# Two-layer graph attention on one core: the projections of a pair parted at other places, the end written in the loop's order, evictions reordered

## Chip, cores, metric

One Trainium2 chip, one NeuronCore. The metric is device time in microseconds of one execution; the profile is one execution, taken by the hardware profiler.

## The reference

128 graphs of 128 nodes with 256 features. Layer 0: `x = x + adj @ (h @ W0) + b0`. Layer 1 is an 8-head graph attention. In both, `h = max(layernorm(x), 0)`.

```python
feat_proj = (feats @ fc_w + fc_b).reshape(bs, n, HEADS, dim).transpose(0, 2, 1, 3)
q = feat_proj @ q_w + q_b
k = feat_proj @ k_w + k_b
logits = q + jnp.swapaxes(k, -1, -2)
masked = logits + (1.0 - adj_mat[:, None]) * NEG
masked = jax.nn.leaky_relu(masked, negative_slope=0.01)
attn = jax.nn.softmax(masked, axis=-1)
out = attn @ feat_proj
out = out.transpose(0, 2, 1, 3).reshape(bs, n, HEADS * dim)
out = out @ fp_w + fp_b + feats
return jax.nn.sigmoid(out)
```

## The kernel before

The graphs are taken in 64 pairs. At the start (begin(), `fold`) fc_w and fp_w are multiplied into one matrix per head, so that each pair needs `g = h @ m` (8 heads of 256 columns for each of its two graphs) and then `y = sum over heads of attn @ g`. Every fp32 product is written as three matmuls of split operands (high and low part, `split`, L400 to L405), and every result that is an operand later is evicted twice: its high part by ScalarE (ACT: `g_high`, `last_high`, `pT_high`, `hT_high`, `ah_high`), its low part by VectorE (DVE: `g_low`, `last_low`, `pT_low`, `hT_low`, `ah_rest`).

Names of a pair's work. `aggregate` (L449) and `transform` make layer 0's output; `residual0`, `stats1`, `mean1` and GpSimd's `variance1` to `shift1` and ACT's `h1_relu` make h; `transpose_h` turns it. `last_head` multiplies the eighth head together with the key and query columns; j is the graph of the pair. `turn_keys` transposes the keys, DVE's `key_rows_out` copies them (L855), SyncE (SP) writes them to DRAM (`keys_out`) and reads them back into all partitions (`keys_in`, L303); GpSimd's (POOL) `mask_keys` (L1617) adds the mask, DVE's `mask_min` (L881) the query, then `leaky` (L888), ACT's `exp` (L1300), DVE's `inverse`, POOL's `normalise` (L1624), PE's `transpose_p` (L521), `pT_high` and `pT_low`, and PE's `attend`, each for one graph j and one half c of the heads. DVE's `add_feats`, ACT's `tanh` and `sigmoid`, POOL's `residual1` and SP's `store` end a pair.

The projections of a pair are six pieces of 512 columns, A0, A1, A2 of the first graph and B0, B1, B2 of the second, six matmuls each (36 in all), and SIXTH, 12 matmuls of 256 columns. They share four PSUM banks in turn (`RING`, L43): a piece can start when `g_low` or `last_low` of the bank's tenant before it is done (`ring_free`). The tenants of one bank follow each other so: B0 and A0; A1 and B1; A2 and SIXTH; THERE (the second graph's last_head of the pair after) and B2. The transposed attention has one bank (`TRING`): each `transpose_p` waits for the `pT_low` before it.

Every engine's program is a hand-written list, executed in order: begin(), then step(i, q) in a loop over pairs (PE, DVE, ACT for i = 4 to 60, POOL 5 to 58, SP 6 to 59; three steps in one turn of the loop), then finish(). Between engines there are only semaphores. The step of PE: L656 to L678.

Of the kernel before, what the change touches and what calls it, by code (L numbers as in the profile page):

```python
# [12 lines left out]
DT = D // P  # L13
# [5 lines left out]
BANK = 512  # L19
# [22 lines left out]
LAST = (HERE, THERE)  # L42
RING = ((B0, -1), (A1, 0), (A2, 0), (THERE, 1), (A0, 0), (B1, 0), (SIXTH, 0), (B2, 0))  # L43
# [4 lines left out]
def gnn_pair(nc, graph, identity, head_mask, row_coef, w0, bias0, fc_wT, fc_b, qk_w, q_b, k_b, fp_w, fp_b, out):  # L48
# [9 lines left out]
    with ExitStack() as ctx:  # L58
# [188 lines left out]
        def _(sp):  # L247
# [119 lines left out]
            def finish():  # L367

                keys_in(59, 2, 0)
                keys_in(59, 2, 1)  # L370
                load(63, 0)
                keys_out(60, 0)
                store(57)
                keys_in(60, 0, 0)
                keys_in(60, 0, 1)
                keys_out(61, 1)
                store(58)
                keys_in(61, 1, 0)
                keys_in(61, 1, 1)
                keys_out(62, 2)  # L380
                store(59)
                keys_in(62, 2, 0)
                keys_in(62, 2, 1)
                keys_out(63, 0)
                keys_in(63, 0, 0)
                keys_in(63, 0, 1)
                store(60)
# [11 lines left out]
        def _(pe):  # L399
            def split(out_ap, pairs, first=True, last=True):  # L400

                terms = [(w, m) for (wh, wl), (mh, ml) in pairs for w, m in ((wl, mh), (wh, ml), (wh, mh))]
                for n, (w, m) in enumerate(terms):
                    mm = pe.matmul(out_ap, w, m, start=first and n == 0, stop=last and n == len(terms) - 1)  # L404
# [91 lines left out]

            def project(p, q, n):
                bank = ring_free(n, p)
                folded(p)
                j, s = n // 3, slice(n % 3 * BANK, (n % 3 + 1) * BANK)  # L500
                split(bank[:],
                      [((hT_hi[q][:, dt, j, :], hT_lo[q][:, dt, j, :]), (m_hi[:, dt, s], m_lo[:, dt, s]))
                       for dt in range(DT)]).then_inc(pe_g[n], 1)
# [37 lines left out]
            def begin():  # L541
# [109 lines left out]
                transform(5, 2)  # L651
                attend(3, 0, 0, 0)
# [3 lines left out]
            def step(i, q):  # L656
                project(i - 1, (q + 2) % U, B0)
                attend(i - 1, (q + 2) % U, 0, 1)
                transpose_h(i + 1, (q + 1) % U)
                project(i, q, A1)  # L660
# [5 lines left out]
                project(i, q, A0)  # L666
                attend(i - 1, (q + 2) % U, 1, 0)
# [3 lines left out]
                project(i, q, B1)  # L671
# [3 lines left out]
                project(i, q, B2)  # L675
# [4 lines left out]
            def finish():  # L680

                h_ready(60)
                project(60, 0, B0)
                attend(60, 0, 0, 1)
                h_ready(61)
                project(61, 1, A1)
                transpose_p(60, 1, 1)
                transpose_h(62, 2)
# [4 lines left out]
                project(61, 1, A0)  # L693
                attend(60, 0, 1, 0)
                transpose_p(61, 0, 0)
                attend(60, 0, 1, 1)
                turn_keys(62, 2)
                project(61, 1, B1)
                transform(63, 0)
                sixth_heads(61, 1)  # L700
                transpose_p(61, 0, 1)
                project(61, 1, B2)
                attend(61, 1, 0, 0)
                transpose_p(61, 1, 0)
                project(61, 1, B0)
# [1221 lines left out]
```

## Time and profile before

| | us |
|---|---|
| median of 3 runs | 1433.05 (1432.97 to 1435.38) |
| the profiled execution | 1436.59 |
| its span, first to last instruction | 1434.8 |
| its mean granted clock of PE | 0.994 |

In the rows below PE is TensorE, a time is counted from the span's start, a line is that of the kernel before, and `[x <-E tile Ln]` behind an instruction is the engine's idle time ahead of it and what ended it. `x4` behind a merged row counts instructions. A matmul's own duration is longer than its distance to the next, because matmuls are pipelined: distances of starts are what adds up.

### The profile page before, as it was taken

Reading aid. Unit: us, or ns where it says so; the run is one execution under the profiler, and the core shown is the slowest. Engines: PE = TensorE matmul, PEld = TensorE weight load, DVE = VectorE, ACT = ScalarE, POOL = GpSimd, SP = SyncE. Lnnn points to the kernel's source line nnn. Section 1 sums busy time; section 2 is a strip of 40 time slices with the busy share of each in tenths; the row PEclk is TensorE's granted clock in tenths of the full one; section 3 lists DMA queues with packets and bytes.
Section 4 is the critical chain, followed back from the end, with each engine's and each line's share of the span. In section 5 each row is a group of like instructions: output and inputs, shape, how many; then the busy total and the mean of one; then the engine's idle time right before and its main releaser. Section 6 shows DMA issues by size and latency. Waiting matters only on the chain.

```text
span 1434.8 us, 32663 instructions
## 1 busy us (share of the span) xinstructions
PE 1408.9 (98%) x9624; PEld 1296.5 (90%) x9624; DVE 1267.8 (88%) x4536; ACT 1100.5 (77%) x3428; POOL 1105.1 (77%) x1291
## 2 busy tenths in 40 slices
PE   9989999999999999999999999999999999999987
PEld 7878999999999999999999999999999999998876
DVE  7978999999999999999999999999999989998865
ACT  4757877877877877877877877877877877877755
POOL 4768888787787788787788788788778778778744
PEclk9989999999999999999999999999999999999999
DMA  6321332232232232232232231232232232231111
GB/s 223 103 61 63 95 103 69 85 103 70 84 103 67 87 103 71 83 103 69 85 103 69 85 103 70 84 103 72 82 103 71 83 103 74 80 103 61 58 41 56
DMA packets 43245, 123.13 MB, mean 86 GB/s; under 512 B 5968, under 2 KB 9680, under 8 KB 43216
## 3 DMA queue, kind: packets, MB, share of 16 engines
q1 hardware_dynamic: 42928, 122.77, 26.9%
q8 instruction: 13, 0.21, 0.1%
q14 instruction: 16, 0.13, 0.0%
q10 hardware_dynamic: 288, 0.01, 0.0%
HBM read 105.46 MB, written 17.30 MB: 86 GB/s over the span
## 4 chain that ended last, share of the span: by engine, by line
PE 90%; POOL 3%; DVE 3%; issue 2%; DMA 1%; ACT 1%; POOLq 0%; ACTq 0%; DVEq 0%
PE gbank L404 43%; PE ybank L404 23%; PE bank L404 9%; PE tbank L521 7%; PE bank L449 4%; PE bank L479 2%; PE gbank L424 1%; POOL att L1624 1%; POOL att L1617 1%; DVE att L881 1%; DMA late<-key_rows 1%; PE bank L457 0%; DVE g_lo L864 0%; DVE att L888 0%; DMA qk<-qk_w_dram 0%
## 5 line engine op out<-in xcount | busy, mean ns | idle before, releaser
L1617 POOL TENSOR_TENSOR att<-late,t_pos 128x512 f32<-128x512 f32 x256 | 331.1, 1295 | 175.6 <-PE tbank L521 117.0
L1300 ACT ACTIVATE att<-att 128x128 f32<-128x128 f32 x1024 | 397.8, 393 | 50.0 <-DVE att L888 49.7
L404 PE MATMUL gbank<-m_hi,hT_lo 128*128 128x512 f32 (+1 forms) x1024 | 402.4, 393 | 2.1 <-DVE g_lo L864 2.1
L404 PE MATMUL gbank<-m_hi,hT_hi 128*128 128x512 f32 (+1 forms) x1024 | 375.0, 366 | 0.0
L404 PE MATMUL gbank<-m_lo,hT_hi 128*128 128x512 f32 (+1 forms) x1024 | 373.2, 364 | 0.0
L1624 POOL TENSOR_TENSOR att<-att,rinv 128x512 f32<-128x512 f32 x256 | 295.0, 1152 | 63.4 <-DVE rinv L893 63.2
L881 DVE TENSOR_SCALAR_CACHE_REDUCE att<-att,kq_sb 128x128 f32<-128x128 f32 x1024 | 291.5, 341 | 33.1 <-POOL att L1617 32.8
L864 DVE TENSOR_TENSOR g_lo<-gbank,g_hi 128x512 fp32r<-128x512 f32 x448 | 302.5, 679 | 18.2 <-ACT g_hi L1293 14.4
L1307 ACT ACTIVATE pT_hi<-tbank 128x512 fp32r<-128x512 f32 x256 | 152.7, 597 | 178.4 <-PE tbank L521 175.5
L1293 ACT ACTIVATE g_hi<-gbank 128x512 fp32r<-128x512 f32 x448 | 258.7, 592 | 38.7 <-PE gbank L404 38.5
L404 PE MATMUL ybank<-g_hi,pT_lo 128*128 128x256 f32 x889 | 249.7, 281 | 4.4 <-DVE g_lo L864 4.3
L404 PE MATMUL ybank<-g_lo,pT_hi 128*128 128x256 f32 x889 | 249.1, 280 | 0.0
L404 PE MATMUL ybank<-g_hi,pT_hi 128*128 128x256 f32 x889 | 248.8, 280 | 0.0
L404 PEld LDWEIGHTS gbank<-m_hi,hT_hi 128*128 128x128 f32 x1024 | 192.9, 188 | 34.2
L404 PEld LDWEIGHTS gbank<-m_hi,hT_lo 128*128 128x128 f32 x1024 | 193.8, 189 | 21.0 <-DVE g_lo L864 2.3
L404 PEld LDWEIGHTS gbank<-m_lo,hT_hi 128*128 128x128 f32 x1024 | 194.6, 190 | 19.9
L871 DVE TENSOR_TENSOR pT_lo<-tbank,pT_hi 128x512 fp32r<-128x512 f32 x256 | 173.3, 677 | 37.1 <-ACT pT_hi L1307 37.1
L1300 ACT ACTIVATION_READ_ACCUMULATOR att<-att 128x1 f32 x1024 | 194.8, 190 | 0.0
L888 DVE SCALAR_TENSOR_TENSOR att<-att 128x516 f32<-128x516 f32 x256 | 191.4, 766 | 0.1
L404 PEld LDWEIGHTS ybank<-g_hi,pT_lo 128*128 128x128 f32 x889 | 167.4, 188 | 13.0 <-issue 5.4
L404 PEld LDWEIGHTS ybank<-g_lo,pT_hi 128*128 128x128 f32 x889 | 167.4, 188 | 7.6
L404 PEld LDWEIGHTS ybank<-g_hi,pT_hi 128*128 128x128 f32 x889 | 166.9, 188 | 0.0
(123 smaller groups left out, 2876.9 us busy)
## 6 DMA issues: line engine op xcount, KB each, us to landing
late<-key_rows SPq DMA_DIRECT2D x128, 512.0 KB, 6.3
g_in<-graph_dram SPq DMA_DIRECT2D x64, 512.0 KB, 3.3
out_dram<-ends SPq DMA_DIRECT2D x63, 256.0 KB, 6.6
att<-fc_wT_dram SPq DMA_DIRECT2D x4, 256.0 KB, 5.8
late<-fp_w_dram SPq DMA_DIRECT2D x4, 256.0 KB, 5.3
ends<-fp_w_dram SPq DMA_DIRECT2D x2, 512.0 KB, 7.7
late<-fc_wT_dram SPq DMA_DIRECT2D x2, 512.0 KB, 8.4
key_rows<-rows SPq DMA_DIRECT2D x64, 8.0 KB, 1.4
```

Of the source, the lines that this page charges most:

```text
L404: mm = pe.matmul(out_ap, w, m, start=first and n == 0, stop=last and n == len(terms) - 1)
L449: mm = pe.matmul(sums[:, j, dt, :], h0_f[q][:, j, dt * P:(dt + 1) * P], adjT_of(q)[:, j, :], start=True, stop=True)
L521: mm = pe.transpose(tbank[:, h * P:(h + 1) * P], att[j][c][:, h * P:(h + 1) * P], ident[:])
L864: dve.tensor_tensor(piece(g_lo, n), bank_of(n, p), piece(g_hi, n).bitcast(F32), ALU.subtract)\
L871: dve.tensor_tensor(pT_lo[j][:, hs, :], rows, pT_hi[j][:, hs, :].bitcast(F32), ALU.subtract)\
L881: r = dve.tensor_scalar(a[:, s], a[:, s], kq_sb[q][:, 1, j, c * HC + h:c * HC + h + 1], None, ALU.add, ALU.min, accum_out=a[:, CH + h:CH + ...
L888: dve.scalar_tensor_tensor(out=a, in0=a, scalar=SLOPE, in1=a, op0=ALU.mult, op1=ALU.min)\
L1293: act.activation(piece(g_hi, n), bank_of(n, p), ACT.Copy).then_inc(a_g[n], 1)
L1300: e = act.activation(a[:, s], a[:, s], ACT.Exp, scale=-1.0, bias=a[:, CH + h:CH + h + 1], accum_out=esum[j][c][:, h:h + 1])
L1307: act.activation(pT_hi[j][:, c * HC:(c + 1) * HC, :], rows, ACT.Copy).then_inc(a_pT[NC * j + c], 1)
L1617: gp.tensor_tensor(a, keys[q][:, j, c * HC:(c + 1) * HC, :], t_pos[q][:, j, :].unsqueeze(1).broadcast_to([P, HC, P]), ALU.add)\
L1624: gp.tensor_tensor(a, a, rinv[j][c][:].unsqueeze(2).broadcast_to([P, HC, P]), ALU.mult)\
```

## The change

`split` takes a slice of its terms, and `project_part(p, q, n, first, stop)` issues the terms first to stop−1 of a piece's six matmuls; only the part that ends at 6 signals. Each part asks for the bank and for the folded weights as `project` does. In the loop the pieces are parted so: two matmuls of B0 go ahead of attend(i, 0, 0) (and aggregate, transpose_p(i, 1, 0)); one of A1 ahead of attend(i−1, 0, 1) and transpose_h; one of B1 ahead of attend(i−1, 1, 0), attend(i−1, 1, 1), turn_keys and transpose_p(i, 0, 0); two of B2 ahead of sixth_heads, transform and transpose_p(i, 0, 1). The rest of the piece follows where the whole one stood. DVE's step has g_low(i, A1) and pT_low(i−1, 1, 1) ahead of the keys' work, and last_low(i+1, 1) right behind keys_queries(i+1, 1). ACT's has g_high(i, A1) and pT_high(i−1, 1, 1) first. POOL's and SP's steps are unchanged. In begin() PE has B0(3) parted, DVE the work around pair 2 in another order, ACT last_high(3, 0, 1) ahead of exp(2, 0, 1). finish() of all five engines is written in the order of the step, with what no longer exists left out.

The diff, cut to the parts that are spoken of (finish() is shown for PE's first pair, and for SP):

```diff
@@ sync, finish
+                load(63, 0)
                 keys_in(59, 2, 0)
                 keys_in(59, 2, 1)
-                load(63, 0)
+                store(57)
                 keys_out(60, 0)
-                store(57)
                 keys_in(60, 0, 0)
                 keys_in(60, 0, 1)
+                store(58)
                 keys_out(61, 1)
-                store(58)
...
@@ tensor
-            def split(out_ap, pairs, first=True, last=True):
+            def split(out_ap, pairs, first=True, last=True, part=slice(None)):
 
                 terms = [(w, m) for (wh, wl), (mh, ml) in pairs for w, m in ((wl, mh), (wh, ml), (wh, mh))]
-                for n, (w, m) in enumerate(terms):
+                for n, (w, m) in list(enumerate(terms))[part]:
...
+            def piece_terms(q, n, out_ap, part):
+                j, s = n // 3, slice(n % 3 * BANK, (n % 3 + 1) * BANK)
+                return split(out_ap,
+                             [((hT_hi[q][:, dt, j, :], hT_lo[q][:, dt, j, :]), (m_hi[:, dt, s], m_lo[:, dt, s]))
+                              for dt in range(DT)], part=part)
+
+            def project_part(p, q, n, first, stop):
+                bank = ring_free(n, p)
+                folded(p)
+                mm = piece_terms(q, n, bank[:], slice(first, stop))
+                if stop == TERMS:
+                    mm.then_inc(pe_g[n], 1)
...
@@ tensor, begin
                 transform(5, 2)
+                project_part(3, 0, B0, 0, 2)
                 attend(3, 0, 0, 0)
...
             def step(i, q):
-                project(i - 1, (q + 2) % U, B0)
+                project_part(i - 1, (q + 2) % U, B0, 2, 6)
+                project_part(i, q, A1, 0, 1)
                 attend(i - 1, (q + 2) % U, 0, 1)
                 transpose_h(i + 1, (q + 1) % U)
-                project(i, q, A1)
+                project_part(i, q, A1, 1, 6)
                 transpose_p(i - 1, 1, 1)
...
                 project(i, q, A0)
+                project_part(i, q, B1, 0, 1)
                 attend(i - 1, (q + 2) % U, 1, 0)
                 attend(i - 1, (q + 2) % U, 1, 1)
                 turn_keys(i + 1, (q + 1) % U)
                 transpose_p(i, 0, 0)
-                project(i, q, B1)
+                project_part(i, q, B1, 1, 6)
+                project_part(i, q, B2, 0, 2)
                 sixth_heads(i, q)
                 transform(i + 2, (q + 2) % U)
                 transpose_p(i, 0, 1)
-                project(i, q, B2)
+                project_part(i, q, B2, 2, 6)
+                project_part(i, q, B0, 0, 2)
                 attend(i, q, 0, 0)
...
             def finish():
 
-                h_ready(60)
-                project(60, 0, B0)
+                project_part(60, 0, B0, 2, 6)
+                project_part(61, 1, A1, 0, 1)
                 attend(60, 0, 0, 1)
-                h_ready(61)
-                project(61, 1, A1)
+                transpose_h(62, 2)
+                project_part(61, 1, A1, 1, 6)
                 transpose_p(60, 1, 1)
-                transpose_h(62, 2)
                 project(61, 1, A2)
...
@@ vector, begin
                 mask_min(2, 2, 0, 1)
                 mask_min(2, 2, 0, 0)
-                leaky(2, 0, 1)
                 leaky(2, 0, 0)
-                mask_min(2, 2, 1, 0)
                 hT_low(3, 0)
                 pT_low(1, 1, 1)
+                leaky(2, 0, 1)
+                mask_min(2, 2, 1, 0)
                 mask_min(2, 2, 1, 1)
                 inverse(2, 0, 0)
-                g_low(2, A1)
-                ah_rest(4, 1)
-                add_feats(1, 1)
-                inverse(2, 0, 1)
-                leaky(2, 1, 1)
                 keys_queries(3, 0, 0)
                 keys_queries(3, 0, 1)
                 last_low(3, 0, 0)
+                g_low(2, A1)
+                ah_rest(4, 1)
+                leaky(2, 1, 1)
+                inverse(2, 0, 1)
+                add_feats(1, 1)
+                key_rows_out(3)
                 leaky(2, 1, 0)
-                key_rows_out(3)
                 g_low(2, A2)
...
@@ vector, step
                 mask_min(i, q, 1, 1)
+                g_low(i, A1)
+                pT_low(i - 1, 1, 1)
                 keys_queries(i + 1, (q + 1) % U, 0)
                 last_low(i + 1, (q + 1) % U, 0)
                 inverse(i, 0, 0)
                 leaky(i, 0, 1)
                 keys_queries(i + 1, (q + 1) % U, 1)
-                pT_low(i - 1, 1, 1)
-                g_low(i, A1)
+                last_low(i + 1, (q + 1) % U, 1)
                 mask_min(i, q, 1, 0)
...
                 pT_low(i, 0, 0)
-                last_low(i + 1, (q + 1) % U, 1)
                 g_low(i, A0)
...
@@ scalar, begin
                 last_high(3, 0, 0)
+                last_high(3, 0, 1)
                 exp(2, 0, 1)
-                last_high(3, 0, 1)
...
@@ scalar, step
             def step(i, q):
+                g_high(i, A1)
+                pT_high(i - 1, 1, 1)
                 g_high(i, A2)
                 last_high(i + 1, (q + 1) % U, 0)
-                pT_high(i - 1, 1, 1)
-                g_high(i, A1)
                 last_high(i + 1, (q + 1) % U, 1)
```

## Rows read from the trace of the kernel before

**Rows 1.** The page, part 1: busy us (share of span) xinstructions of every engine.
```profile
PE 1408.9 (98%) x9624; PEld 1296.5 (90%) x9624; DVE 1267.8 (88%) x4536; ACT 1100.5 (77%) x3428; POOL 1105.1 (77%) x1291
```

**Rows 2.** Chain of waits, 120 to 1290 us: shares by engine, tile and line.
```profile
by line: PE gbank L404 48.7%; PE ybank L404 26.4%; PE bank L404 10.1%; PE tbank L521 8.1%; PE bank L449 4.2%; PE bank L479 2.0%; PE bank L457 0.5%
```

**Rows 3.** Stretches: us, busy of PE, PEld, DVE, ACT, POOL; granted clock, DMA share, GB/s.
```profile
1272.62:1294.11 21.49, 21.49 (x152) 19.89 (x151) 19.54 (x71) 17.05 (x53) 17.27 (x21) 1.00 0.31 86
...
1294.11:1317.26 23.15, 21.66 (x151) 19.86 (x151) 19.54 (x71) 17.12 (x53) 19.81 (x22) 1.00 0.19 68
...
1338.75:1361.20 22.45, 22.16 (x151) 19.75 (x151) 19.95 (x71) 16.69 (x53) 14.52 (x17) 1.00 0.18 60
...
1361.20:1390.04 28.84, 24.42 (x144) 21.76 (x143) 19.00 (x65) 16.46 (x53) 15.39 (x16) 0.88 0.12 46
...
1390.04:1434.80 44.76, 36.19 (x244) 32.31 (x242) 27.77 (x87) 26.00 (x86) 18.49 (x17) 0.99 0.16 48
```

**Rows 4.** Timeline of PE in begin(): start, us, instruction [idle before <- releaser].
```profile
83.36 0.60 PE L404 MATMUL bank<-n_hi,hT_lo 128*128 128x272 f32 x1 [3.53 <-DVE hT_lo L841]
...
92.48 0.37 PE L457 MATMUL bank<-ident,kq_sb 128*16 128x128 f32 x1 [2.04 <-DVE last_lo L859]
...
111.73 0.39 PE L404 MATMUL bank<-n_hi,hT_lo 128*128 128x272 f32 x1 [1.38 <-DVE hT_lo L841]
```

**Rows 5.** Stretch 85 to 86 us, columns as in Rows 3 (granted clock behind POOL).
```profile
85.00:86.00 1.00, 1.00 (x6) 1.00 (x5) 1.00 (x3) 0.88 (x4) 0.87 (x1) 0.50 0.72 272
```

**Rows 6.** Timeline of PE in one step of the loop.
```profile
705.21 1.05 PE L449 MATMUL bank<-g_in,h_f 128*128 128x128 f32 x8
...
706.10 0.60 PE L521 MATMUL tbank<-ident,att 128*128 128x128 f32 x4
...
706.46 0.48 PE L404 MATMUL gbank<-m_hi,hT_lo 128*128 128x512 f32 x1
...
707.93 0.28 PE L404 MATMUL ybank<-g_hi,pT_lo 128*128 128x256 f32 x1
...
709.35 0.60 PE L479 MATMUL bank<-ident,h 128*128 128x128 f32 x4
...
713.00 0.28 PE L404 MATMUL bank<-n_hi,hT_lo 128*128 128x272 f32 x1
...
713.74 0.29 PE L404 MATMUL gbank<-n_hi,hT_lo 128*128 128x272 f32 x1
```

**Rows 7.** Timeline of DVE in the same step.
```profile
707.37 0.69 DVE L871 TENSOR_TENSOR pT_lo<-tbank,pT_hi 128x512 fp32r<-128x512 f32 x1 [0.46 <-ACT pT_hi L1307]
...
711.02 0.68 DVE L841 TENSOR_TENSOR hT_lo<-bank,hT_hi 128x512 fp32r<-128x512 f32 x1
...
713.27 0.35 DVE L881 TENSOR_SCALAR_CACHE_REDUCE att<-att,kq_sb 128x128 f32<-128x128 f32 x1 [0.51 <-POOL att L1617]
...
714.87 0.85 DVE L888 SCALAR_TENSOR_TENSOR att<-att 128x516 f32<-128x516 f32 x1
...
719.84 0.27 DVE L855 COPY rows<-bank 16x128 f32<-16x128 f32 x1
```

**Rows 8.** DVE, ACT and POOL in begin() (timelines); then a piece of the chain.
```profile
78.19 3.45 DVE L888 SCALAR_TENSOR_TENSOR att<-att 128x516 f32<-128x516 f32 x2
...
79.04 0.60 ACT L1285 ACTIVATE hT_hi<-bank 128x512 fp32r<-128x512 f32 x1
...
79.36 1.72 POOL L1607 TENSOR_TENSOR xb<-g_in,b_row 128x512 f32<-128x512 f32 x1
...
81.64 1.06 DVE att L881 x8
```

**Rows 9.** Timeline of PE: its last matmul.
```profile
1430.19 0.28 PE L404 MATMUL bank<-last_hi,pT_hi 128*128 128x256 f32 x1
```

**Rows 10.** Timeline of POOL: mask_keys of the two steps after Rows 7.
```profile
728.24 1.29 POOL L1617 TENSOR_TENSOR att<-late,t_pos 128x512 f32<-128x512 f32 x1 [1.44 <-DMA late<-key_rows]
...
748.95 1.28 POOL L1617 TENSOR_TENSOR att<-late,t_pos 128x512 f32<-128x512 f32 x1 [0.66 <-DMA late<-key_rows]
```

More of the change, by code:

```diff
@@ L499, in project @@
                 folded(p)
[L500 to L503, printed above, removed]
+                piece_terms(q, n, bank[:], slice(None)).then_inc(pe_g[n], 1)
+            def project_part(p, q, n, first, stop):
[4 more added lines that the diff above has]
+                    mm.then_inc(pe_g[n], 1)
             def sixth_heads(p, q):
@@ L1144, in finish @@
             def finish():
-                mask_min(61, 1, 0, 1)
                 g_low(60, SIXTH)
@@ L1153, in finish @@
                 leaky(61, 0, 0)
-                mask_min(61, 1, 1, 0)
                 hT_low(62, 2)
-                leaky(61, 1, 0)
-                leaky(61, 0, 1)
-                inverse(61, 0, 0)
+                mask_min(61, 1, 0, 1)
+                mask_min(61, 1, 1, 1)
+                g_low(61, A1)
                 pT_low(60, 1, 1)
@@ L1192, in finish @@
-                inverse(62, 0, 0)
                 keys_queries(63, 0, 0)
                 last_low(63, 0, 0)
+                inverse(62, 0, 0)
+                leaky(62, 0, 1)
                 keys_queries(63, 0, 1)
-                g_low(62, A1)
+                last_low(63, 0, 1)
+                mask_min(62, 2, 1, 0)
+                inverse(62, 0, 1)
                 g_low(62, A2)
-                mask_min(62, 2, 1, 1)
                 add_feats(61, 1)
                 key_rows_out(63)
-                last_low(63, 0, 1)
@@ L1222, in finish @@
                 leaky(63, 0, 1)
                 mask_min(63, 0, 1, 0)
+                inverse(63, 0, 1)
+                g_low(63, A2)
+                add_feats(62, 2)
                 leaky(63, 1, 0)
-                inverse(63, 0, 1)
-                mask_min(63, 0, 1, 1)
+                leaky(63, 1, 1)
                 pT_low(63, 0, 0)
-                leaky(63, 1, 1)
+                g_low(63, A0)
                 inverse(63, 1, 0)
-                g_low(63, A0)
-                add_feats(62, 2)
@@ L1232, in finish @@
-                inverse(63, 1, 1)
                 pT_low(63, 0, 1)
                 g_low(63, B1)
+                g_low(63, SIXTH)
+                inverse(63, 1, 1)
                 pT_low(63, 1, 0)
-                g_low(63, SIXTH)
                 g_low(63, B0)
```

209 lines of the change are left out of this document (111 added, 98 removed).

## Prediction

> **What bounds the kernel now.** First the page: TensorE (PE) is busy 1408.9 of 1434.8 us, 98% [rows 1]. That is an average over three stages, so next the chain of waits between 120 and 1290 us: every line named there is PE's [rows 2]. Then the stretches cut at one fixed point of every step, the start of `last_head(…, 1)`: a step of the loop is 21.49 us long with PE busy 21.49 [rows 3]. In the loop PE never waits; only fewer or shorter PE instructions, or a new wait, could change it. The idle time is at the two ends. In the loop's last steps and behind it PE stands idle (length less busy) 1.5 us in the step that ends at 1317.26, 0.3 in the one that ends at 1361.20, 4.4 in the next and 8.6 in the final stretch (4.3 of that is the tail), and the clock column reads 0.88 in one of them [rows 3]. In begin() PE waits 3.53 us at 83.36 and 1.38 at 111.73 for hT_lo, and 2.04 at 92.48 before turn_keys [rows 4]. The first of these also costs clock: 85 to 86 is at 0.50, that is 1.2 GHz [rows 5].
>
> **Part 1: the parted projections in the loop, 0.** The same 36 matmuls, weight loads and boundaries remain. A projection behind a transposition takes 1.47 us (706.46 to 707.93) [rows 6], and five blocks of 512 columns still follow a transposition per step; five times a 512-column run is still followed by a 256- or 272-column one. So nothing is saved and nothing added on PE. What moves is the filler between: before attend(i−1, 0, 1) and attend(i−1, 1, 0) one matmul of the next piece is put (0.23 us, a sixth of 1.39), before sixth_heads and attend(i, 0, 0) two (0.46). The pieces end when they did; attends, transform, aggregate and transposes in between start 0.23 or 0.46 later. The added waits are repeats, or ask earlier for a bank: B1's head asks for g_low(A1) ahead of two attends instead of behind them, B2's head for last_low(…, 1) before sixth_heads. The diff brings both forward on VectorE (DVE). Queued behind such a wait would be all of PE.
>
> I walk one new step through the queues to see whether one of these becomes a wait. transpose_p(1, 0) is 0.46 later, so pT_low ends and mask_min(0, 0) starts 0.46 later than in [rows 7]; hT_low, at 711.02 to 711.70, ends at about 712.15, and PE wants it at 713.00 [rows 6]: 0.85 left of 1.3. DVE idles 0.51 at 713.27, waiting for mask_keys(1, 1), which hangs on PE's transpose_p(1, 1), not moved; so the delay is swallowed there [rows 7]. Next come g_low(A1), done by about 715.0 where B1's head starts at 715.9 (713.74 + 0.76 + 1.39), and pT_low(1, 1), 0.6 later for an attend that starts at 717.5. leaky(0, 1) falls back by 1.2, so exp(0, 1) ends near 718.4 and DVE may wait some 0.3 for it at inverse(0, 1). With last_low(…, 1), 0.34 issue to issue, now in front, rows is copied some 0.5 later than 719.84 [rows 7]. g_low(A2) has 2 us left before sixth_heads, normalise(0, 0) on GpSimd (POOL), 1.0 later than now, 1.3 before its transposition. The smallest distance left is about 0.65 us. Hence 0 in all 57 steps; the bounds are 0 and, from the keys' loop below, +0.18 us a step.
>
> **Part 2: begin(), −7.8 us.** DVE's work for pair 2 is reordered. Now hT_low(3) is behind both leaky(2, 0, ·), 3.45 us for two, and mask_min(2, 1, 0), 1.06 [rows 8]. In the new order only leaky(2, 0, 0) is ahead of it: 78.19 plus half of 3.45 is 79.9, past the end of hT_hi at 79.64, so hT_lo (0.68, its last part overlapping) is there at 80.55 and PE goes on at 80.6 instead of 83.36. It has idled 0.9 us instead of 3.5. After 1.38 idle the row at 111.73 is followed by full speed, after 3.53 the clock was halved [rows 4, 5]; I take full clock. last_head ×2 and project(2, A0) take 2.9, attend 1.42: PE reaches turn_keys(3) at 84.9. Ahead of last_low(3, 0) DVE has pT_low, leaky(2, 0, 1) (1.7 again, beside POOL's input work), two mask_min, inverse and keys_queries: 81.1 + 1.7 + 2.1 + 0.25 + 0.35 = 85.5. So turn_keys runs at 85.65, against 92.48: 6.8 sooner. From there by the same durations: B1 waits for g_low(2, A1), 86.2; sixth_heads(2) for g_low(2, A2), which stands behind ah_rest, leaky, add_feats, rows and leaky, 89.5; B2 to 92.35; B0 94.2; attend(2, 0, 1) waits for g_low(SIXTH), 96.2; then A1, two transposes, A2 and an attend to 102.7; hT_low(4), behind mask_min, leaky, g_low, mask_min and pT_low, ends at 103.9. The wait before last_head(4, 0) remains (1.25 us), but the point is 103.95 instead of 111.73 [rows 4]: −7.8. POOL and the keys of pair 3 come 7.0 sooner or more. Bounds: −4 (the clock falls once more, 1.3 to 1.9, and the two waits behind turn_keys grow) and −9 (those waits vanish).
>
> **Part 3: finish() in the loop's order, −15.5 us.** POOL's and SyncE's (SP's) finish take over from step 59 on. If the loop's order holds there, steps 59 and 60 take 21.49. Step 61 lacks aggregate, 0.89 (705.21 to 706.10) [rows 6]: 20.6. Step 62 lacks transform too, 12 matmuls of 256 columns as in an attend, 1.42 (707.93 to 709.35): 19.2. PE's own work from the tail of B0(62) to the end, item by item in the new list (a matmul of 512 columns 0.23, attend and sixth_heads 1.42): 1.0 + 0.23 + 1.42 + 1.16 + 0.44 + 2.77 + 0.23 + 2.83 + 0.44 + 1.24 + 0.46 + 1.42 + 0.44 + 1.0 + 0.46 + 1.42 + 0.44 + 1.0 + 1.42 + 0.44 + 2.83 = 23.1, where 0.44 is four transposes with what the next 512 columns lose behind them. I add 0.35 because B1's head of pair 63 waits for g_low(63, A1): that pair's step is shorter and its keys come by DMA. 23.4. The last stage, from the end of the last attend, is untouched: 1430.47 to 1434.80, 4.3 [rows 9]. The start of step 58's B0 tail is 713.74 − 706.92 = 6.8 before its cut at 1294.11, 1287.3. Sum: 1287.3 + 3 × 21.49 + 20.6 + 19.2 + 23.4 + 4.3 = 1419.3 against 1434.8: −15.5. By stretches of [rows 3] that is 1.7 of the one to 1317.26, 1.0 of the one to 1361.20, 8.2 of the next (28.84 against 20.6) and 4.7 of the last. Bounds: −16 (no wait at all) and −11 (the last stretch keeps what it loses now).
>
> **The sum.** 1434.8 − 7.8 − 15.5 = 1411.5 us of span. The profiled run took 1436.59, 1.8 more than its span and 3.5 more than the median of 1433.05; the same difference of 23.3 taken from the median gives 1409.8, and that is the forecast.
>
> **Rivals.**
> (a) Begin's gain is mostly given back: the keys of pair 3 or a clock drop set PE's next stop. For it: three waits follow each other there, and I resolve them to about 0.5 us each. Against it: everything behind 92.48 hangs on DVE work that moves along. Begin then gives −2 and the time is 1415.6.
> (b) The keys' loop takes the step over. From the copy of rows to mask_keys 8.40 us (719.84 to 728.24) [rows 7, 10], mask_keys with the hand-over to DVE 1.33, DVE's work to the next copy 11.25 without its idle 0.51: 20.98. The change adds last_low 0.34 and up to 0.33 of waiting for exp: 21.67, 0.18 over 21.49. For it: the sum. Against it: 8.40 is not every step's: the next copy, 21.49 later at 741.33, is followed by mask_keys at 748.95, 7.62 [rows 10]; the mean of the two is 0.39 less. If it holds, 57 × 0.18 less the 0.9 of distance is +9: 1419.
> (c) Slower: leaky(0, 1), (1, 0) and (1, 1) land on POOL's normalise and mask_keys. In the loop leaky(0, 1) takes 0.85 [rows 7], in begin() beside POOL's input work 1.7 each, while POOL's xb takes 1.72 [rows 8]. Were all four of a step to take 1.7, DVE would need up to 4 us more; it has 1.95 of idle (21.49 − 19.54) [rows 3]. It decides from 1.95 + 23.3/57 = 2.36 us a step on; at 3 us a step the loop gives +60, the total 1470. Against it: in [rows 7] leaky meets POOL already and loses 0.25.
> (d) The orders outside the loop do nothing, since the ends wait for DMA: 1433.
>
> By the Trainium skill (SBUF — State Buffer, "Who interferes with whom") a DVE instruction with two SBUF inputs and a GpSimd instruction that reads SBUF exclude each other, and the later one blocks for the whole of the other. leaky is such an instruction, and 1.7 us in [rows 8] agree in kind. By that rule each overlap could cost up to one POOL instruction, 1.3 us, which is rival (c).
>
> **Chances.** Forecast 0.70 (own range 1405 to 1416), (a) 0.11, (b) 0.11, (c) 0.06, (d) 0.02. The range leaves out (c), (d) and the far ends of the others: 1404 to 1421. About 0.2% (3 us) is what a measurement of this kernel can tell from no change. Faster by more 0.92, within it 0.02, slower by more 0.06.
>
> **What would show it.** In the profile after: the loop's step still 21.49 with PE busy 21.49; if it is longer, the idle row names hT_lo or g_lo at `last_head` or at B1's head, and POOL's wait for late<-key_rows near zero would show (b), leaky above 1.2 us (c). The wait for hT_lo near 80 under 1.2 us, turn_keys(3) near 85.7 and last_head(4, 0) near 104 show part 2. Idle of PE behind the loop, the tail aside, of about 0.4 us instead of 10.5 shows part 3, and its clock full until the end. The forecast is wrong if one of the distances of part 1, 0.65 us at the least, is used up in every step, or if the last pairs' keys, 6 us on their way, stop PE in step 62 or 63.

## The result, and the profile after

| | before | after |
|---|---|---|
| median, us | 1433.36 (1432.97 to 1435.38, 4 runs) | 1397.97 (1397.29 to 1399.49, 4 runs) |
| the profiled execution | 1436.59 | 1399.49 |
| its span | 1434.8 | 1397.7 |

The ratio is 0.975 (95% interval 0.9735 to 0.9769): 35.4 us less, where 23.3 were forecast. 1398 lies outside the range of 1404 to 1421.

The page of the kernel after, part 1, against [rows 1]:

```profile
PE 1386.2 (99%) x9624; PEld 1276.7 (91%) x9624; DVE 1289.3 (92%) x4536; ACT 1092.9 (78%) x3428; POOL 1123.7 (80%) x1291
```

PE's waits in it for hT_lo, the normalised attention, g_lo and last_lo (us in total, times, longest):

```profile
PE bank L405 <- DVE hT_lo L867: 2.6, 3, 1.4
...
PE tbank L532 <- POOL att L1650: 0.7, 2, 0.5
PE gbank L405 <- DVE g_lo L890: 0.6, 1, 0.6
PE bank L458 <- DVE last_lo L885: 0.2, 1, 0.2
```

PE has the same 9624 matmuls and is busy 22.7 us less with them. That is the first sign: idle time that is removed leaves the busy time as it is.

Where the 37.1 us of span went. The timeline of PE in begin(), kernel after, beside [rows 4]:

```profile
80.74 0.39 PE L405 MATMUL bank<-n_hi,hT_lo 128*128 128x272 f32 x1 [0.81 <-DVE hT_lo L867]
...
85.15 0.27 PE L458 MATMUL bank<-ident,kq_sb 128*16 128x128 f32 x1
...
103.45 0.39 PE L405 MATMUL bank<-n_hi,hT_lo 128*128 128x272 f32 x1 [1.43 <-DVE hT_lo L867]
```

And the stretches of the kernel after, cut at the starts of last_head(…, 1) (columns as in [rows 3]):

```profile
1251.92:1273.15 21.23, 21.23 (x151) 19.64 (x150) 19.93 (x71) 16.92 (x55) 17.57 (x21) 1.00 0.29 87
1273.15:1294.39 21.24, 21.24 (x152) 19.65 (x150) 19.93 (x71) 16.95 (x55) 17.56 (x21) 1.00 0.29 87
...
1315.62:1336.85 21.23, 21.23 (x151) 19.65 (x150) 19.21 (x66) 16.93 (x55) 17.41 (x20) 1.00 0.19 63
1336.85:1357.20 20.35, 20.35 (x144) 18.77 (x143) 18.89 (x66) 15.71 (x52) 15.97 (x17) 1.00 0.21 66
1357.20:1397.70 40.50, 35.61 (x245) 32.25 (x243) 28.86 (x93) 27.17 (x88) 20.11 (x18) 0.98 0.16 47
...
84.00:86.00 2.00, 2.00 (x16) 1.80 (x15) 2.00 (x9) 0.48 (x4) 1.24 (x2) 1.00 0.87 223
```

- Begin: last_head(4, 0) at 103.45 instead of 111.73, 8.3 sooner. The clock is 1.00 where it was 0.50 [rows 5].
- Loop: from there to the start of last_head(59, 1) at 1293.94 (the cut of [rows 3] at 1294.11 lies 0.17 behind it) were 1182.2 us, in 55 steps; to the same point at 1273.15 are 1169.7 now. 12.5 less. The usual step is 21.23 instead of 21.49, with PE busy in all of it, before and after.
- End: 140.9 us were left, 124.55 are. 16.3 less.

8.3 + 12.5 + 16.3 = 37.1. The loop's 12.5 is what the forecast had at nothing.

In the loop no wait is gone, since there was none [rows 3]. The same matmuls stand closer together. The timeline of PE in one step of the kernel after: sixth_heads from 727.57, transform from 728.93, transpose_p, B2's tail and B0's head, attend(i, 0, 0) from 732.11, the aggregate, and in the next step attend(i−1, 0, 1), the one of [rows 6], from 736.02:

```profile
727.34 0.39 PE L405 MATMUL gbank<-m_lo,hT_hi 128*128 128x512 f32 x1
727.57 0.28 PE L405 MATMUL gbank<-m_hi,hT_lo 128*128 128x256 f32 x1
...
728.93 0.28 PE L405 MATMUL bank<-w_hi,ah_lo 128*128 128x256 f32 x1
...
730.30 0.60 PE L532 MATMUL tbank<-ident,att 128*128 128x128 f32 x4
730.65 0.47 PE L405 MATMUL gbank<-m_hi,hT_hi 128*128 128x512 f32 x1
...
732.11 0.28 PE L405 MATMUL ybank<-g_hi,pT_lo 128*128 128x256 f32 x1
...
733.52 1.05 PE L450 MATMUL bank<-g_in,h_f 128*128 128x128 f32 x8
...
736.02 0.28 PE L405 MATMUL ybank<-g_hi,pT_lo 128*128 128x256 f32 x1
...
737.38 0.60 PE L480 MATMUL bank<-ident,h 128*128 128x128 f32 x4
```

Twelve matmuls of 256 columns took 1.42 in [rows 6] (707.93 to 709.35). Here they take 1.36 in attend(i−1, 0, 1), in sixth_heads and in transform, but 1.41 in attend(i, 0, 0). The two attends on graph 1, 24 matmuls, take 2.72 instead of 2.82 (743.92 to 746.64, against 715.88 to 718.70). So 60 of the 72 matmuls of 256 columns in a step go at 113.3 ns from start to start instead of 117.8, and 60 × 4.5 ns = 0.27 is the step's 0.26.

What sets the pace shows in the matmuls of 512 columns ahead. The rows round to 10 ns; the trace has the starts in ns. The distances from each 512-column matmul to what follows it, where not said otherwise behind four transpositions, and the pace of the 256-column run behind (one group for each; the entry, the first two or three distances, varies from step to step):

```
before, attend(i-1,0,1), 6 ahead:  318 232 237 231 232 226            -> 117.8
after,  attend(i-1,0,1), 5 ahead:  319 231 237 232 231                -> 113.3
before, sixth_heads,     6 ahead:  317 235 230 231 226 229            -> 117.8
after,  sixth_heads,     7 ahead:  319 235 229 231 226 229 232        -> 113.3
after,  attend(i,0,0),   6 ahead:  313 226 229 231 226 229            -> 117.8
before, attend(i,0,0),   6 ahead:  318 235 229 232 226 229            -> 117.8
after,  attend(i-1,1,*), 7 ahead:  232 226 229 232 226 229 231 (no transposition between) -> 113.3
```

The distances fall into a beat of three, 226, 229, 232 ns. Where the last one is 231 or 232, the 256-column run behind it goes at 113.3; otherwise at 117.8. A run keeps its pace to its end: 12 matmuls in a row, or 24.

The theory for the experiments: it is the number of 512-column matmuls between the last transposition and a 256-column run, taken in this beat, that sets the run's pace. Before, all cuts were at the ends of pieces of six, and a six always ended on the wrong beat: of the four runs in each of 54 steps of the loop none was fast. After, three of the four are fast in 53 or 54 steps, and attend(i, 0, 0) in none. Its rivals: parity (odd counts fast), the neighbours (what VectorE, ScalarE and GpSimd read and write meanwhile), any parting at all, the new order of the evictions, and the ends.

### The profile page after: what moved, and what is told of

The parts are those of the page before. It is cut to its first block, busy times and chain, and to the rows that moved or that the text cites. A ratio compares the mean times of both kernels' runs of the same rounds, so it can differ in the third digit from the quotient of the medians.

```text
span 1397.7 us, 32661 instructions
## 1 busy us (share of the span) xinstructions
PE 1386.2 (99%) x9624; PEld 1276.7 (91%) x9624; DVE 1289.3 (92%) x4536; ACT 1092.9 (78%) x3428; POOL 1123.7 (80%) x1291
## 4 chain that ended last, share of the span: by engine, by line
PE 93%; POOL 2%; DVE 2%; issue 2%; ACT 1%; DMA 0%; POOLq 0%; ACTq 0%; DVEq 0%
PE gbank L405 45%; PE ybank L405 23%; PE bank L405 10%; PE tbank L532 8%; PE bank L450 4%; PE bank L480 2%; PE gbank L425 1%; POOL att L1650 1%; POOL att L1643 1%; DVE att L907 1%; PE bank L458 0%; ACT att L1326 0%; DMA qk<-qk_w_dram 0%; DVE att L914 0%; ACT g_hi L1319 0%
## 5 line engine op out<-in xcount | busy, mean ns | idle before, releaser
L405 PE MATMUL gbank<-m_hi,hT_hi 128*128 128x512 f32 (+1 forms) x1024 | 383.1, 374 | 0.0
L405 PE MATMUL gbank<-m_hi,hT_lo 128*128 128x512 f32 (+1 forms) x1024 | 378.6, 370 | 0.6 <-DVE g_lo L890 0.6
L405 PE MATMUL gbank<-m_lo,hT_hi 128*128 128x512 f32 (+1 forms) x1024 | 379.1, 373 | 0.0
L1650 POOL TENSOR_TENSOR att<-att,rinv 128x512 f32<-128x512 f32 x256 | 290.7, 1136 | 82.2 <-DVE rinv L919 81.9
L1319 ACT ACTIVATE g_hi<-gbank 128x512 fp32r<-128x512 f32 x448 | 255.0, 585 | 6.5 <-PE gbank L405 6.4
L914 DVE SCALAR_TENSOR_TENSOR att<-att 128x516 f32<-128x516 f32 x256 | 209.8, 838 | 0.1
```

What stands on the lines that cost most here:

```text
L914: dve.scalar_tensor_tensor(out=a, in0=a, scalar=SLOPE, in1=a, op0=ALU.mult, op1=ALU.min)\
L1319: act.activation(piece(g_hi, n), bank_of(n, p), ACT.Copy).then_inc(a_g[n], 1)
L1650: gp.tensor_tensor(a, a, rinv[j][c][:].unsqueeze(2).broadcast_to([P, HC, P]), ALU.mult)\
```

## The beat measured by itself

The changed kernel with a row of matmuls behind its end, all other engines idle:

```diff
+            def bench():
+                for n in list(range(10)) + list(range(9, -1, -1)):
+                    turn4()
+                    wide(n)        # n matmuls of 512 columns
+                    half()         # 12 matmuls of 256 columns
+                for n in range(1, 10):
+                    wide(n)
+                    half()
...
             finish()
+            bench()
```

> The changed kernel with a row of matmuls appended on PE once everything else is done (other engines idle, no waits inside): groups of four transposes, n matmuls of 512 columns, 12 matmuls of 256 columns, for n = 0 to 9 and back, then other orders; the appended part is not to be counted in the time. It measures the distance of the 256-column matmuls, 113.3 ns in the runs after 5 and 7 matmuls in the loop of the changed kernel and 117.8 ns everywhere in the loop of the kernel before. Theory, beat of three: in runs of 512-column matmuls the distances repeat as 226, 229, 232 ns, and a 256-column run goes at 113.3 ns if it begins behind a 232, at 117.8 otherwise; so behind four transposes n = 4 and 7 are fast, 5, 6 and 8 slow, and without transposes every third n is fast. Rival, parity: odd n fast, even n slow. Rival, neighbours: the distance is set by what the other engines read and write meanwhile, so with all of them idle every run shows the same distance, whatever n.

The stretch of the first loop but for its last run (columns as above):

```profile
1409.40:1465.30 55.90, 55.90 (x395) 51.97 (x394) 0.00 (x0) 0.00 (x0) 0.00 (x0) 1.00 0.00 1
```

From the timeline the groups without transpositions, n = 1, 2 and 3 (L788 is a matmul of 512 columns, L794 one of 256):

```profile
1467.14 0.39 PE L788 MATMUL gbank<-m_hi,hT_lo 128*128 128x512 f32 x1
1467.36 0.28 PE L794 MATMUL ybank<-g_hi,pT_lo 128*128 128x256 f32 x1
...
1468.78 0.39 PE L788 MATMUL gbank<-m_hi,hT_lo 128*128 128x512 f32 x1
1469.01 0.39 PE L788 MATMUL gbank<-m_lo,hT_hi 128*128 128x512 f32 x1
1469.24 0.28 PE L794 MATMUL ybank<-g_hi,pT_lo 128*128 128x256 f32 x1
...
1470.60 0.39 PE L788 MATMUL gbank<-m_hi,hT_lo 128*128 128x512 f32 x1
```

No other engine is busy, the clock is 1.00, and both paces are there: 1467.36 to 1468.78 is 1.42, 1469.24 to 1470.60 is 1.36. That ends the neighbours' theory. In ns, without a transposition between the groups:

```
n  distances of the n matmuls              12 x 256 behind
1  226                                     117.8
2  230 231                                 113.3
3  226 229 232                             113.4
4  226 229 232 225                         117.8
5  229 232 225 230 231                     113.3
6  226 229 232 226 229 232                 113.3
7  225 230 231 226 229 232 226             117.8
8  229 232 226 229 231 226 229 232         113.4
9  226 229 232 226 229 231 226 229 232     113.4
```

Behind a fast group the beat starts at 225 or 226, behind a slow one at 229 or 230 (the first row stands behind a run that itself followed transpositions); a run is fast when the count ends it at 231 or 232. That makes six of nine counts fast, not every third, as I had expected: each run's pace moves the start of the next beat. Every third it is where the start stays the same: behind last_head's 272-column matmuls, where the first distance is always 231 or 232, n = 1, 4 and 7 are fast (113.3 to 113.4), 2, 3, 5, 6 and 8 slow (117.7 to 118.0). Parity is out: 3 and 5 are fast, 1 and 7 slow, 2, 6 and 8 fast. The operands are out too: with one and the same weights and columns in all n matmuls, 4 and 7 are fast, 3, 5, 6 and 8 slow. With four transpositions ahead the first distance is 312 to 319 and the beat comes in at different places:

```
entry 312..313:  313 226 229 232 226 229       n = 4 fast, 3 and 6 slow
entry 315..316:  316 226 233 236 229 232       n = 6 fast, 4 and 5 slow
entry 318, 235:  318 235 229 232 226 229 232   n = 4 and 7 fast, 3, 5, 6 and 8 slow
entry 319, 231:  319 231 237 232 231 226 229   n = 5 fast, 3 and 7 slow
```

So "n = 4 and 7 are fast, 5, 6 and 8 slow" was only half right: the entry depends on what went before the transpositions, and n = 4, 5, 6 and 7 were each seen fast and slow. What holds, with few exceptions, is the rule on the last distance. Over the thirteen traces here (twelve kernels, the changed one twice) there are 3307 runs of eight or more 256-column matmuls behind two or more of 512: with a last distance of 231 to 233, 1617 of 1654 were fast; with any other, 23 of 1653. Three of the exceptions stand in this bench, behind 318, 232, 237, 231 and twice behind 316, 226, 233. 60 matmuls of 256 columns in a row, begun slow, stayed at 117.8 to the end.

## The loop, the ends, and any parting at all

The loop's part of the change alone, on the kernel before (step() of PE, DVE and ACT; B0's first two matmuls of pair 3 in begin() so that the loop can start):

```diff
 begin, PE of the kernel before
+                project_part(3, 0, B0, 0, 2)
                 attend(3, 0, 0, 0)
 finish, PE of the kernel before
-                project(60, 0, B0)
+                project_part(60, 0, B0, 2, 6)
```

> The kernel before with only the loop's part of the change: step() of TensorE, VectorE and ScalarE as in the changed kernel, and B0's two first matmuls of pair 3 ahead of attend(3, 0, 0); begin() and finish() of every engine otherwise as before. Theory (four of the five groups of 256-column runs of a step run at 113.3 instead of 117.8 ns a matmul, 60 matmuls): a step takes 21.23 instead of 21.49 us, 57 steps give 14.8, so about 1418.5 us. The forecast's theory (nothing saved in the loop): 21.49 a step, 1433. Rival, the step is shorter only because the ends start it in another rhythm: 1433 too, with 21.49 a step here.

Measured: 1421.83 us (1418.92 to 1425.75, 5 runs), ratio 0.9905 (0.9875 to 0.9934), 13.6 us less by the ratio; a step is 21.23. The loop alone makes the loop's gain.

Its profile says two things more. Begin() is the old one, yet last_head(4, 0) stood at 105.90 in this execution, not at 111.73: the wait for hT_lo ended at 81.44 after 2.42 us, and the clock stayed up (timeline of PE, then a stretch, columns as above):

```profile
81.44 0.40 PE L405 MATMUL bank<-n_hi,hT_lo 128*128 128x272 f32 x1 [2.42 <-DVE hT_lo L857]
```

```profile
84.00:86.00 2.00, 2.00 (x15) 1.74 (x13) 0.32 (x1) 0.70 (x4) 0.40 (x1) 1.00 0.94 326
```

So of begin's 8.3 us in the profiles some 5.8 belong to a late and half-clocked stretch that not every execution has. And from the start of last_head(59, 0) the loop's last steps with the old finish() take 146.3 us to the end, where they took 141.6 in the profile of before. PE's wait for the normalised attention in the first of its steps is 2.08 instead of 1.49. Part of what the loop gains is given back there.

The complement, begin() and finish() as changed, step() of PE, DVE and ACT as before:

> The complement: the changed kernel with step() of TensorE, VectorE and ScalarE as before, and B0 of pair 3 and of pair 60 whole; begin() and finish() as changed. Theory: begin gives 8 (turn_keys(3) at about 85, last_head(4, 0) at about 103.5), finish 13 to 14, the loop keeps 21.49 a step: about 1412 us. By the forecast's theory this is the whole change: 1433.4 - 23.3 = 1410. If the ends gave the whole of the measured 35 us by setting the loop's rhythm: 1398.

Measured: 1412.32 us (1411.92 to 1413.14, 4 runs), ratio 0.9839 (0.9806 to 0.9871), by the ratio 23.1 less than before beside it; a step is 21.49; last_head(4, 0) stands at 103.07. These are the parts that the forecast had in its sum, at the size it had them. Beside finish()'s 16.3 that leaves some 7 us for begin(), an estimate from these figures: the old begin()'s late stretch seems to be in most executions, though it was not in the profiled one of the loop alone. The two halves, 13.6 and 23.1, give 36.7; the whole is 35.4, well within what their intervals leave open.

All four heads two matmuls long:

```diff
-                project_part(i, q, A1, 0, 1)
+                project_part(i, q, A1, 0, 2)
...
-                project_part(i, q, B1, 0, 1)
+                project_part(i, q, B1, 0, 2)
```

> The changed kernel with two matmuls of the next piece ahead at all four places (B0 2, A1 2, B1 2, B2 2), in the loop and in the ends; one matmul more ahead than now for A1 and B1, nothing else. Counts of 512-column matmuls since the last transposition ahead of a 256-column run: 6, 8 behind last_head, 6 and 6, where the changed kernel has 5, 7, 7 and 6. Theory (the count decides whether a run goes at 113.3 or 117.8 ns): all runs slow, 21.49 a step, 1398 + 15 = 1413 us. Rival, any parting of the pieces shortens the step (shorter groups of 512 columns, filler between): 21.23, 1398 us. Rival, the reordered evictions do it: 21.23, 1398 us.

Measured: 1412.29 us (1411.76 to 1413.39, 4 runs), ratio 0.9837 (0.9804 to 0.9869). One matmul more ahead at two places, and the loop's gain is gone: 21.49 a step. It isn't the parting, but where it cuts. The profile shows all groups slow, with 6, 8, 6 and 6 ahead.

Nothing parted, evictions and ends in the new order:

```diff
-                project_part(i - 1, (q + 2) % U, B0, 2, 6)
-                project_part(i, q, A1, 0, 1)
+                project(i - 1, (q + 2) % U, B0)
...
-                project_part(i, q, B1, 0, 1)
```

> The changed kernel with nothing parted: all pieces whole, in loop and ends; the new order of evictions and of the ends stays. Theory (the order of evictions gives nothing by itself, the counts are 6 everywhere): 21.49 a step, about 1412.5 us. Rival (the evictions' order gives the loop's gain): 21.23, 1398.

Measured: 1412.83 us (1412.16 to 1413.28, 4 runs), ratio 0.9844 (0.9827 to 0.9861). The new order of the evictions gives nothing by itself.

The stretches of one step in the middle of each of the four, the last line of the view (PE, then the other engines, busy):

```profile
sum 21.23, PE 21.23 PEld 19.64 DVE 19.95 ACT 16.94 POOL 17.57; mean PE 21.23 PEld 19.64 DVE 19.95 ACT 16.94 POOL 17.57
```

```profile
sum 21.48, PE 21.48 PEld 19.89 DVE 19.53 ACT 17.05 POOL 17.25; mean PE 21.48 PEld 19.89 DVE 19.53 ACT 17.05 POOL 17.25
```

```profile
sum 21.49, PE 21.49 PEld 19.90 DVE 19.95 ACT 16.93 POOL 17.61; mean PE 21.49 PEld 19.90 DVE 19.95 ACT 16.93 POOL 17.61
```

```profile
sum 21.48, PE 21.48 PEld 19.89 DVE 19.93 ACT 17.11 POOL 17.55; mean PE 21.48 PEld 19.89 DVE 19.93 ACT 17.11 POOL 17.55
```

They are the loop alone, the ends alone, all heads two, and whole pieces, in this order. PE is busy all of the step in each; only the length differs.

## What the order of the evictions is for

The changed kernel with the loop's evictions in the old order (VectorE's step is shown, ScalarE's goes back likewise):

```diff
 vector, step
-                g_low(i, A1)
-                pT_low(i - 1, 1, 1)
                 keys_queries(i + 1, (q + 1) % U, 0)
...
+                pT_low(i - 1, 1, 1)
+                g_low(i, A1)
-                last_low(i + 1, (q + 1) % U, 1)
...
                 pT_low(i, 0, 0)
+                last_low(i + 1, (q + 1) % U, 1)
```

> The changed kernel with VectorE's and ScalarE's step() as in the kernel before: the pieces parted as in the change, the loop's evictions in the old order. B1's head asks for g_low(A1), which in the old order ends 1.1 us behind the point where the head stands (716.97 against 715.88 in the step shown of before), and B2's head for last_low(..., 1), which ends at 722.4 where the head stands at about 720.2, 721.3 with the first wait. Theory (order of the evictions is what keeps the new parts free of waits): two waits of about 1.1 us each in every step, some 23.4 us a step, the total near 1520; the 256-column runs behind a wait may lose the fast pace too. Rival (the parts need no new order, the old one has slack): 21.23 a step, 1398.

PE's longest waits in its profile:

```profile
PE gbank L405 <- DVE last_lo L885: 82.1, 57, 1.7
PE gbank L405 <- DVE g_lo L890: 58.4, 58, 1.0
```

Measured: 1580.04 us (1579.64 to 1580.39, 4 runs), ratio 1.101 (1.0993 to 1.1031). The two waits are the expected ones, 1.0 and 1.4 us a step. I had 1520: the step is 24.44, 3.2 more than 21.23, not 2.2. Beside the 2.45 of idle time, the distances at the two waits (1411 and 1887 ns at 712.5 and 718.6 us, where 229 would stand without one) are 0.33 longer than their idle time of 1.01 and 1.50, the matmul behind each has 340 ns to the next instead of 229 (0.22 for both), and the runs of 24 behind a wait mostly fell to the slow pace (48 × 4.5 ns = 0.22). A head ahead of time asks for its bank ahead of time; without the new order the change would have cost 146 us.

## Four other cuts

```diff
 five_seven, against the changed kernel
-                project_part(i, q, B0, 0, 2)
+                project_part(i, q, B0, 0, 3)
-                project_part(i, q, A1, 0, 1)
+                project_part(i, q, A1, 0, 2)
 four_eight: no head of B0, A1 0 to 2
 four_seven: B0 0 to 3, A1 0 to 1
 seven_four: no head of B0, A1 0 to 1
```

> The changed kernel with three matmuls of B0 instead of two ahead of attend(i, 0, 0) and two of A1 instead of one ahead of attend(i-1, 0, 1), in the loop and the ends. Counts since the last transposition ahead of the 256-column runs become 7 before attend(i, 0, 0), where it is 6 now, and 5, 7, 7 at the three others, as now. Theory, beat of three: the last slow run of the step, attend(i, 0, 0), goes fast as well, 12 matmuls by 4.5 ns, 0.055 a step: 21.18 us, total about 1395. The parity rival expects the same here. If the fast pace went with the operands or the place in the step and not with the count: 1398.

> The changed kernel with no matmul of B0 ahead of attend(i, 0, 0) and two of A1 ahead of attend(i-1, 0, 1): B0 whole, B2 and B1 parted as now. Counts since the last transposition: 4 before attend(i, 0, 0), 8 before attend(i-1, 0, 1), 7 and 7 at the others. Theory, beat of three: behind the entry that the trace shows for four transposes and the aggregate (318, 232, 237, 231, 232, then 226, 229, 232), the eighth distance is a 232, and the fourth in attend(i, 0, 0)'s (313, 226, 229, 232) as well: all five places fast, 21.18 a step, about 1395 us. Rival, parity: both even, both slow, 21.28 a step, about 1401 us.

Measured: 1397.11 us (1395.97 to 1397.89, 4 runs), ratio 0.9735 (0.9718 to 0.9753), for 7 and 5; and 1396.03 (1395.48 to 1396.87, 4 runs), ratio 0.973 (0.9713 to 0.9748), for 4 and 8. A step is 21.21 in each, not the 21.18 that I gave. attend(i, 0, 0) did go fast, with 7 ahead in the one and 4 in the other, as the beat has it (parity would have it slow with 4). But attend(i−1, 0, 1) fell to the slow pace, with 5 and 8 ahead: the transpositions behind the aggregate were now followed by 312 or 313 instead of 318 or 319, and with that entry the fifth and the eighth matmul end on 226. A group that goes fast changes where the next one comes in. From the same table the fourth and the seventh are right there:

> The changed kernel with three matmuls of B0 instead of two ahead of attend(i, 0, 0), nothing else: counts since the last transposition 7 before attend(i, 0, 0), 4 before attend(i-1, 0, 1), 7 and 7. In the run with counts 7 and 5 attend(i, 0, 0) went fast, and the transpositions behind the aggregate were then followed by distances of 313, 226, 229, 232 instead of 319, 231, 237, 232, 231, so that the fifth matmul was no longer the right one, the fourth is. Theory (three-beat, and the group before sets the entry behind the transpositions): all five places fast, 60 matmuls + 12, another 0.055 us a step against the changed kernel and 0.025 for the shorter entry, 21.15 us, about 4 us less than the changed kernel run beside it. Rival (only two or three of the places can be fast at once, as in the two runs before): 21.21, 1 to 2 us less.

> The changed kernel with no matmul of B0 ahead of attend(i, 0, 0) (B0 whole), nothing else: counts since the last transposition 4 before attend(i, 0, 0), 7 before attend(i-1, 0, 1), 7 and 7. Theory as for the run with 7 and 4: behind the entry 313, both the fourth and the seventh matmul are followed by 232, so all places fast, 21.15 us a step, about 4 us less than the changed kernel beside it. Parity would make attend(i, 0, 0) slow here (4) and leave 21.23.

> The changed kernel as it is, for a comparison on the same chip: 1398 us, 21.23 a step, ratio to the kernel before 0.975.

| run beside each other | median, us (5 runs each) | ratio, 95% | step |
|---|---|---|---|
| 7 before attend(i, 0, 0), 4 before attend(i−1, 0, 1) | 1396.65 (1395.54 to 1397.72) | 0.9735 (0.9715 to 0.9755) | 21.15 |
| 4 and 7 | 1397.32 (1395.03 to 1398.81) | 0.9738 (0.9716 to 0.9759) | 21.15 |
| the changed kernel | 1400.19 (1398.92 to 1402.85) | 0.9761 (0.974 to 0.9783) | 21.23 |

```profile
sum 21.16, PE 21.16 PEld 19.59 DVE 19.85 ACT 16.90 POOL 17.56; mean PE 21.16 PEld 19.59 DVE 19.85 ACT 16.90 POOL 17.56
```

That is a step with 7 and 4. All 72 matmuls of 256 columns go at 113.3, the usual step is 21.15 as said, and the medians are 3.5 and 2.9 us below the changed kernel's, near the expected 4. The ratios' intervals overlap; the five times of each do not overlap with the changed kernel's. So three matmuls of B0 ahead instead of two is the better cut by these runs, by 0.2%, but that the fifth place gives it is not shown in the totals: 5 and 7, and 4 and 8, with one slow place left, came out as low beside the kernel before. In the profiled executions the loop's 55 steps take 1167.0 us with 7 and 4 and 1166.5 with 4 and 7, but also 1166.5 with 4 and 8 and 1167.6 with 7 and 5, against 1170.2 for the changed kernel beside them and 1168.9 for its first profile. What the shorter usual step gains was in part lost again in 13 and 11 single steps of these two that were longer, as is told below for the changed kernel.

## Why the prediction was wrong, point by point

**What bounds the kernel.** Right: PE in the loop, with no wait before and one of 0.36 us after. The text says that "only fewer or shorter PE instructions, or a new wait, could change it", and then looks for new waits only.

**Part 1, the loop at 0.** This is the step that failed. "The same 36 matmuls, weight loads and boundaries remain", "so nothing is saved and nothing added on PE" takes the duration of a matmul as a property of its shape. It is a property of the shape and of where its run begins in the beat of those before it. The size of the error is 12.5 us of span: 55 steps × 0.256 = 14.1, less 1.3 in five steps that were 0.13 to 0.52 longer and 0.2 in the first step. It explains nearly all of the 13.8 that the span gained beyond the forecast. My bounds for this part, 0 to +0.18 a step, left no room below nothing. The trace of before could have shown it: in finish(), twelve 512-column matmuls stand ahead of an attend, and it goes at the fast pace (timeline of PE, kernel before):

```profile
1402.47 0.39 PE L404 MATMUL gbank<-m_hi,hT_hi 128*128 128x512 f32 x1
1402.70 0.28 PE L404 MATMUL ybank<-g_hi,pT_lo 128*128 128x256 f32 x1
...
1403.95 0.28 PE L404 MATMUL ybank<-g_hi,pT_hi 128*128 128x256 f32 x1
```

From the first to the twelfth, eleven distances, are 1.25 us, 113.6 ns each. In [rows 6] the group of twelve is 1.42, 118 each. The spread of such groups over the whole trace, in place of one of them, would have put up to 72 × 4.5 ns = 0.32 a step into the bounds, 18 us for 57 steps.

The longest of the five longer steps ends with 753 ns instead of 229 ahead of last_head, and the trace shows why (timelines of POOL, DVE and PE, kernel after):

```profile
1076.12 1.29 POOL L1643 TENSOR_TENSOR att<-late,t_pos 128x512 f32<-128x512 f32 x1 [2.71 <-DMA late<-key_rows]
...
1077.44 0.35 DVE L907 TENSOR_SCALAR_CACHE_REDUCE att<-att,kq_sb 128x128 f32<-128x128 f32 x1 [1.33 <-POOL att L1643]
...
1081.05 0.40 PE L405 MATMUL bank<-n_hi,hT_lo 128*128 128x272 f32 x1 [0.36 <-DVE hT_lo L867]
```

The keys came late in this one step, so GpSimd's mask_keys was late, with it DVE's mask_min and the hT_lo behind it, and PE stood idle for hT_lo; the step behind it has its run of 24 slow, behind distances of 231 to 235 ns that are out of the beat (one of the exceptions to the rule). The same three waits stand one behind the other in the longest steps of the runs with 7 and 4, 4 and 7, and of the changed kernel again, each time with 2.0 us or more for the keys (1.5 or 1.6 at about 141 us).

The other half of Part 1 was right but for that: in the usual step none of the new waits came. DVE in a step of the kernel after:

```profile
725.01 0.18 DVE L919 RECIPROCAL rinv<-esum 128x4 f32<-128x4 f32 x1 [0.24 <-ACT att L1326]
...
726.88 0.27 DVE L881 COPY rows<-bank 16x128 f32<-16x128 f32 x1
727.08 1.96 DVE L914 SCALAR_TENSOR_TENSOR att<-att 128x516 f32<-128x516 f32 x2
```

The wait for exp at the inverse is 0.24 where I had 0.3. B1's head found g_low(A1) done and B2's head last_low(…, 1), because DVE does both early; without that order the step is 3.2 us longer.

**Part 2, begin(), −7.8.** Right by its places: 80.74 (forecast 80.6) behind 0.81 of idle time (the text has 0.9, where its own times give 0.77), turn_keys at 85.15 (85.65), last_head(4, 0) at 103.45 (103.95), −8.3. By its size only against that one profile of before: where the old begin() escapes the clock's fall, as in the run of the loop alone, the same point stands at 105.90, and the new begin() is worth 2.5 us there. I took the profiled execution's begin for every execution's.

**Part 3, finish(), −15.5.** Right. By stretches I had 1.7, 0, 1.0, 8.2 and 4.7; measured from one start of last_head(…, 1) to the next are 1.9, 0.2, 1.2, 8.5 and 4.4, 16.3 in all (rounded), of which 0.8 is the faster pace in three steps. Without it 15.5 is left, the forecast to the tenth; that close a hit is luck, since single terms are off by up to 0.3 and the cut it started from by 0.17.

**Rivals.** (a) Begin's gain given back: no. (b) The keys' loop: the sum that spoke for it held in part, GpSimd's waits for the keys are 58.7 us where they were 58.5, in steps that are 0.26 shorter. PE waited for them once, by way of DVE, as shown above; DVE's own waits for mask_keys fell from 32.8 us to 4.8, so the distance that the change left is small. (20.98 + 0.34 + 0.33 is 21.65, not 21.67: 0.16 a step.) (c) leaky against GpSimd: there, and small. Two leaky took 1.96 instead of 1.43 and the mean of all 256 went from 766 to 838 ns, 0.3 us a step, and with it DVE's busy time from 19.54 to 19.93; the 2.36 us from which it would decide were far off. What is left of the GpSimd instruction under way sets the price: a leaky that starts 0.27 us before its end takes 0.82 (720.04, kernel before), with 0.80 left 1.35 (727.08, kernel after, beside the normalise below), with 1.23 left 1.78 (78.19 in begin() of before), each time what is left and 0.55; with none under way it takes 0.68.

```profile
726.84 1.04 POOL L1650 TENSOR_TENSOR att<-att,rinv 128x512 f32<-128x512 f32 x1
```

The Trainium skill's rule that the two exclude each other and the later one blocks (SBUF — State Buffer, "Who interferes with whom") agrees with these numbers. (d) The orders outside the loop do nothing: no, they give 21 to 24 us (whole pieces, ends alone).

## What to carry to other kernels

Where an engine is busy all of the time and never waits, look at the distances of its instructions by group, all over the trace: the same shape can have two paces, and which it has can hang on the number of instructions ahead of it. A change that only moves a cut is then not free of cost or gain, and trying each count is cheap. And a part that is issued early asks for its buffer early: what frees the buffer has to move with it.

## What the hardware showed

- A run of 256-column matmuls (fp32r, with a weight load for each) goes at 113.3 or 117.8 ns from start to start at the same granted clock of 1.00, with all other engines idle too. The Trainium skill (TensorE: Matmul & The Clock Gate, "Back-to-back issue gap") gives one gap for each size; by its formula for a single gap an estimate for 256 columns is 109 ns. The runs show two paces, both above it.
- 512-column matmuls of this kind repeat 226, 229, 232 ns, 229 on the mean.
- Behind four transpositions the first 512-column matmul has 312 to 319 ns to the next. Which of them it is changes with what went before: behind attend(i, 0, 0), the aggregate and transpositions it is nearly always 318 or 319 where attend(i, 0, 0) was slow and 312 or 313 where it was fast. In the bench it was 316, 318 or 319 behind fast runs, and anything from 312 to 319 behind slow ones.
- A `leaky` (two SBUF inputs) that starts beside a GpSimd instruction lasts 0.55 us longer than that instruction's rest: 0.82, 1.35 and 1.78 us with 0.27, 0.80 and 1.23 left.
- Why there is a beat, and why it has three, no run here tells. The counts with other column numbers, or with other weight loads, were not tried.
- PE stood idle for 2.42 us in one execution without a fall of the clock, and for 3.53 us in another with the clock at 0.50, 1.2 GHz, behind it [rows 5].
